# A second matrix of filter taps, with rows of 16, for the blocks that read the first one from an odd column

## The reference

```
k = jnp.transpose(kernel, (1, 2, 0))[:, :, None, :]
y = lax.conv_general_dilated(x, k, window_strides=(1, 1), padding='SAME',
                             dimension_numbers=('NHWC', 'HWIO', 'NHWC'), feature_group_count=ch)
return x + y
```

## Time and profile before

| | |
|---|---|
| median of 3 runs | 846.07 us (845.48 to 846.51) |
| the profiled execution | 845.39 us |
| its span, first to last instruction | 843.4 us |
| TensorE, matmuls | 832.9 us busy, 99% |
| VectorE | 728.6 us busy, 86% |
| ScalarE | 617.9 us busy, 73% |
| GpSimd | 248.5 us busy, 29% |
| HBM traffic over the span | 365 GB/s |

### The profile page before, as it was taken

One profiled execution on the slowest core, in us unless ns is written; L12 is line 12 of the kernel. 1 busy time (PEld: TensorE's weight loads), 2 busy tenths in 40 slices (PEclk: granted clock), 3 DMA queues, 4 the chain that ended last, 5 costly groups with the idle time before them and its releaser, 6 DMA issues.

```text
span 843.4 us, 20670 instructions
## 1 busy us (share of the span) xinstructions
PE 832.9 (99%) x7200; PEld 832.7 (99%) x7200; DVE 728.6 (86%) x2212; ACT 617.9 (73%) x1442; POOL 248.5 (29%) x460
## 2 busy tenths in 40 slices
PE   6999999999999999999999999999999999999998
PEld 6999999999999999999999999999999999999998
DVE  6888888888888888888888888888888888888886
ACT  5777677777767777777767777776777777776775
POOL 5223322323133231322323222223223231332310
PEclk9999999999999999999999999999999999999999
DMA  9999999999999999999999999999999999999965
GB/s 375 406 422 361 372 376 362 376 358 387 368 368 370 372 377 371 362 373 378 370 365 368 369 374 371 373 371 382 365 360 380 368 370 373 369 370 376 374 265 223
DMA packets 28615, 309.29 MB, mean 367 GB/s; under 512 B 3168, under 2 KB 3296, under 8 KB 4064
## 3 DMA queue, kind: packets, MB, share of 16 engines
q1 hardware_dynamic: 28512, 307.98, 97.3%
HBM read 158.55 MB, written 149.42 MB: 365 GB/s over the span
## 4 chain that ended last, share of the span: by engine, by line
PE 99%; POOL 0%; DMA 0%; issue 0%; ACT 0%; DVE 0%; DVEq 0%
PE sums L373 66%; PE sums L369 33%; DMA first<-consts 0%; POOL matrix L228 0%; POOL expanded L217 0%; POOL taps L207 0%; POOL spare L204 0%; POOL taps L201 0%; ACT y_out L259 0%; DVE y_out L313 0%; DVEq L92 0%
## 5 line engine op out<-in xcount | busy, mean ns | idle before, releaser
L373 PE MATMUL sums<-matrix,x_high 121*128 121x240 f32 (+3 forms) x4800 | 832.4, 282 | 0.0
L373 PEld LDWEIGHTS sums<-matrix,x_high 121*128 121x128 f32 x4800 | 738.1, 192 | 0.0
L369 PE MATMUL sums<-matrix,x_low 121*128 121x240 f32 (+3 forms) x2400 | 674.6, 281 | 7.0 <-POOL matrix L228 7.0
L259 ACT ACTIVATE y_out<-sums 128x99 f32<-128x99 f32 (+6 forms) x1248 | 416.6, 379 | 216.4 <-PE sums L373 196.2
L369 PEld LDWEIGHTS sums<-matrix,x_low 121*128 121x128 f32 x2400 | 461.0, 192 | 7.0 <-POOL matrix L228 7.0
L313 DVE TENSOR_TENSOR y_out<-sums,y_out 128x60 f32<-128x60 f32 (+6 forms) x1824 | 360.1, 228 | 101.5 <-ACT y_out L259 16.2
L296 DVE TENSOR_TENSOR x_low<-x_in,x_high 121x1280 fp32r<-121x1280 f32 (+1 forms) x288 | 366.3, 1272 | 5.3 <-ACT x_high L249 2.0
L228 POOL TENSOR_TENSOR matrix<-expanded,first 121x300 fp32r<-121x300 f32 x192 | 131.5, 706 | 559.9 <-PE sums L373 559.7
L249 ACT ACTIVATE x_high<-x_in 121x1280 fp32r<-121x1280 f32 x192 | 245.0, 1276 | 5.2 <-DMA x_in<-x 5.2
L217 POOL TENSOR_TENSOR expanded<-taps,first 121x100 f32<-121x100 f32 x192 | 85.3, 464 | 7.5
L287 DVE CAST x_high<-x_in 121x640 fp32r<-121x640 f32 x96 | 47.1, 490 | 4.3 <-DMA x_in<-x 3.7
(11 more groups left out here) (2 smaller groups left out, 0.2 us busy)
## 6 DMA issues: line engine op xcount, KB each, us to landing
x_in<-x SPq DMA_DIRECT2D x95, 1600.0 KB, 10.6
y<-y_out SPq DMA_DIRECT2D x95, 1520.0 KB, 12.3
x_in<-x SPq DMA_DIRECT2D x2, 640.0 KB, 5.0
rest<-later SPq DMA_DIRECT2D x1, 1150.0 KB, 11.4
y<-y_out SPq DMA_DIRECT2D x1, 852.5 KB, 3.5
y<-y_out SPq DMA_DIRECT2D x1, 365.0 KB, 2.3
x_in<-x SPq DMA_DIRECT2D x1, 320.0 KB, 3.0
y<-y_out SPq DMA_DIRECT2D x1, 302.5 KB, 2.6
```

The source lines that it names most:

```text
L259: act.activation(outputs(c, rows, cols), sums(c, t, rows, cols), ACT.Copy).then_inc(copied, 1)
L369: pe.matmul(target, x_low[c % SLOTS][0:PIXELS, at:at + IMAGES], window(c, strip, k, slice(HIGH, HIGH + 1)).squeeze(1), start=k == tile["sq ...
L373: product = pe.matmul(target, x_high[c % SLOTS][0:PIXELS, at:at + IMAGES], window(c, strip, k, slice(part, part + 1)).squeeze(1), start=Fa ...
```

## The change

GpSimd writes a second tensor, `turned`, beside `matrix`. It holds columns 1 to 16 of each of the 15 rows, so its rows are `EVEN` = 16 elements long, and what stood at column 1 of `matrix` stands at column 0. `window()` takes `matrix` where `left` is even (squares 1 and 3) and `turned`, at `left - 1`, where it is odd (squares 0, 2 and 4: from columns 2, 0 and 0). Each channel's `matrix_step` goes up by 6 in place of 4, and TensorE waits for all six before a channel.

```diff
 ROW = 4 * TAPS
+EVEN = SQUARE + 2 * HALO + 1
 MATRIX = REACH * ROW
+TURNED = REACH * EVEN
...
         matrix = [sbuf(f"matrix{i}", [P, 2, MATRIX], F32R) for i in range(SLOTS)]
+        turned = [sbuf(f"turned{i}", [P, 2, TURNED], F32R) for i in range(SLOTS)]
...
-                    pool.wait_ge(matrix_step, 4 * GROUP * group)
+                    pool.wait_ge(matrix_step, 6 * GROUP * group)
...
             def make_matrix(c):
                 if c:
-                    pool.wait_ge(matrix_step, 4 * c)
+                    pool.wait_ge(matrix_step, 6 * c)
...
-                pool.wait_ge(matrix_step, 4 * c + 2)
+                pool.wait_ge(matrix_step, 6 * c + 2)
...
+                    shape = [PIXELS, REACH // TAPS, TAPS, EVEN]
+                    pool.tensor_tensor(
+                        turned[c % SLOTS][0:PIXELS, part, :].rearrange("p (b d q) -> p b d q", d=TAPS, q=EVEN),
+                        expanded[0:PIXELS, part, :].rearrange("p (d q) -> p d q", q=ROW)[:, :, 1:1 + EVEN]
+                        .unsqueeze(1).broadcast_to(shape),
+                        down.rearrange("p (b d) -> p b d", d=TAPS).unsqueeze(3).broadcast_to(shape),
+                        ALU.mult).then_inc(matrix_step, 1)
...
-                grid = matrix[c % SLOTS][0:PIXELS, parts, :].rearrange("p a (h w) -> p a h w", w=ROW)
+                source, row = (matrix, ROW) if left % 2 == 0 else (turned, EVEN)
+                left -= left % 2
+                grid = source[c % SLOTS][0:PIXELS, parts, :].rearrange("p a (h w) -> p a h w", w=row)
...
-                pe.wait_ge(matrix_step, 4 * (c + 1))
+                pe.wait_ge(matrix_step, 6 * (c + 1))
```

## The result

The changed kernel takes 858.14 us (median, 857.13 to 858.56) against 846.09 us before. The ratio is 1.014 with an interval of 1.0128 to 1.0152. The prediction said 825.7 us, with a range from 820.5 to 833.

What follows compares the result with a forecast made beforehand. TensorE's own pace was taken as the bound: the profiled 845.39 us, less 21.1 for faster reads, plus 1.2 at the start, gave 825.5; 825.7 us was forecast, range 820.5 to 833.

Steps and rivals of the forecast that it cites:

- What bounds the kernel: Steady state: nothing feeds TensorE too late, so its own pace, 8.65 us a channel, is the time.
- TensorE's reads: Matmuls and weight loads: reading from even columns takes a channel from 8.65 to 8.43 us, a gain of 21.1 us.
- My rival that the column is not the cause: Square 2's matmuls: something else of square 2 makes it slow, so no gain, 846.6 us; chance 0.06.
- GpSimd's instructions: Two new writes a channel on GpSimd: 0.60 us each, 115 us in all, costing nothing in the steady state.
- the cover: Next channel's matrices on GpSimd: still ready 5 us early; without this slack each channel would pay 1.20 us.
- The start: Before TensorE's first load: it waits for two more writes, 1.2 us, bounds 0.8 and 2.2 us.
- DMA: Loads and stores of a channel: the rate rises from 371 to 381 GB/s, which the queue can follow.
- The rival's "3 times in all": Rival that only part is won, 836.6 us, chance 0.08; against it, only 3 DMA waits, none after the start.
- VectorE: Its work in a channel grows by 0.08 to 7.67 us against 8.43, 0.76 us free: costs nothing.
- the cover at the banks: Seam additions free banks that TensorE wants eight tiles later, more than 4 us.
- The rival "VectorE becomes the bound": GpSimd's new writes hold VectorE for their whole length, 8.79 us a channel, 860.0 us; chance 0.03.
- the point of decision: In the VectorE rival: it decides the time from 1.06 us a channel of added VectorE work on.

Runs made afterwards that it cites:

- the grouped kernel: The changed kernel with each strip's seam additions reordered, first all along the rows, then all along the columns: 822.7 us, ratio 0.9732 to the kernel before.
- the cast on ScalarE: The changed kernel with the high part of the first strip made on ScalarE in place of VectorE: 823.09 us, ratio 0.9735.
- the run without later writes: The changed kernel, but GpSimd writes `turned` in the first two channels only and later squares read old taps: 857.77 us, ratio 1.0146.
- the run with the shifted wait: The changed kernel, `turned` written in two channels only, GpSimd also waiting for VectorE's last low part of the channel ahead: 841.75 us, ratio 0.9953.

## Why the prediction was wrong, point by point

*What bounds the kernel: right.* TensorE alone set 8.65 us. Relieving VectorE changed nothing (846.48 us), and loading GpSimd changed the start alone (847.37).

*TensorE's reads: right, and slightly undervalued.* The step said 8.43 us a channel and a gain of 21.1 us. With the other engines out of the way it is 8.40, and the grouped kernel is 23.1 us under before (845.84 on its chip), where the step and the start together had promised 19.9. Of the 3.2 us more, 2.9 are the 0.03 us a channel, and the start takes 1.3 back; what is left is within the 1.7 us by which that kernel's four executions differ (822.31 to 824.02). The forecast rests on the column. My rival that the column is not the cause would have given 846.6 there.

*GpSimd's instructions: right in the bare length, wrong in the sum.* 0.61 us where nothing is beside them, 0.60 forecast. But one of each two met a low part and took up to 1.86 us, so that they are 1.15 us on the mean and GpSimd is busy for 478 us, not 365. For TensorE the cover held: the matrices are ready about 4.8 us early (7.0 before).

*The start: about right, in part by luck.* 8.48 us in place of 6.99, 1.5 us more against 1.2 forecast. In the experiments the same writes delay the first weight load by anything from 1.0 us (7.97, the cast on ScalarE) to 2.6 us (9.60, the run without later writes), past the bound of 2.2.

*DMA: right.* 382 GB/s in the grouped kernel, 381 forecast. (The rival's "3 times in all" counts ScalarE's waits for a DMA only; the trace has two more of VectorE and one of GpSimd, all at the start.)

*VectorE: this is the step that failed.* It read: "VectorE has 728.6 / 96 = 7.59 us of work in a channel, 7.67 then, against a channel of 8.43: still 0.76 us free. It costs nothing." Busy time was taken for demand. VectorE's instructions in a channel are 23, and the shortest distance of starts seen at each of the 23 places in the kernel before adds up to 8.45 us (0.52 for the high part, 0.74 for the small low part, 2.80 for the two of 1280 columns and 4.40 for the 19 additions). So 0.20 us was free before, and at TensorE's new 8.40 us nothing is. The step put the cover at the banks at "more than 4 us" besides, and it was 2.0 to 2.1. And it had the place of the collision wrong: the small low part stayed at 0.85 us on the mean (0.91 forecast), and the high part and the last low part grew. Of the 36 us between the 822 that TensorE allows and the 858 measured, the run with the shifted wait splits off the parts: 841.75 - 822.7 = 19 us are VectorE's row of instructions with light disturbances, in a run without the new writes, and 857.77 - 841.75 = 16 us come from GpSimd's writes meeting a low part. The new writes themselves added 858.1 - 857.8, next to nothing, since they replaced one collision by another: in the changed kernel the high part and the last low part are longer by 0.12 us each, in the run without the writes the last low part by 0.22 and the high part by 0.02.

*The rival "VectorE becomes the bound": the right engine for the wrong reason, at 0.03.* Its 860.0 us is near 858.1 by accident. It priced the new instructions at 1.20 us and set the point of decision 1.06 us away; the point was passed by TensorE's own gain of 0.25. The rule on mutual exclusion (the Trainium skill, "SBUF — State Buffer", section "Who interferes with whom": the later of the two waits for a whole instruction) I had read as harmless from one row. The rows above agree with it in both directions: VectorE's low part 0.22 us longer (0.35 us of GpSimd's first write were left when it began), GpSimd's write 1.25 us longer. The one that began later paid in both, so VectorE pays only once GpSimd's write begins ahead of its low part.

*Why it came late and stayed.* TensorE ran fast until its lead over VectorE was used up: the margin at the first bank of a channel was 1.67 us in the third channel and 0.15 in the eighth, and it stayed there. Meanwhile GpSimd's first write, which in the kernel before begins some 1.64 us after the start of the last low part, moved towards that start: 1.07 us after it for the fourth channel's matrix, 0.12 for the eighth's, and from the ninth's on always ahead of it, by 0.2 to 0.9 us. From then on VectorE's low part waits too, where before only GpSimd's write had. Why the phase stays there is argued, not shown by a run of its own: GpSimd is released by TensorE's channel end, TensorE by VectorE's additions, and with no margin left that release keeps a fixed distance to VectorE's row of instructions.

## What to carry to other kernels

An engine's demand is the shortest distance from its first to its last instruction of a round when it waits for no other engine; take it from starts in the timeline, since waits on its own results count and busy time leaves them out. Before making the bounding engine faster, compute that for the next one. If the two lie within a few per cent, look also at which instructions of other engines hold it up when they meet, and by how little they miss each other now, because the new pace moves them.

## What the runs showed of the hardware

- A matmul whose moving operand is read in rows of 16 floats costs about 7.5 ns a row from columns 0 and 4 of a row of 20, and about 9.0 from columns 1, 2 and 3 (134 to 137 ns for 15 rows); even and odd do not matter. Rows of 14 cost 7.2 to 7.7 ns from columns 1 to 4. The Trainium skill, "TensorE: Matmul & The Clock Gate", section "Step-by-step: what each phase is for", lets only the number of columns count; 208 elements at 97 or 118 ns and 210 elements at 110 ns contradict that. The Trainium skill, "SBUF — State Buffer", section "Specifications (TRN2)", has lines of 16 bytes and a penalty for each new line crossed; rows of 16 agree with it (four lines or five), and rows of 14 from column 3, five lines as well, do not. Why these are spared stays open.
- So the second matrix serves square 2 alone. For the 14 wide squares 0 and 4 it changes nothing that a run here could show.
- Weight loads of 128 columns go by at 111.7 ns on the mean where nothing else is seen to hold them (single distances go down to 108), 8.38 us for 75. A matmul of 15 rows from column 0 takes 110 to 115 ns where loads are halved. So in the middle strips the two are about equal, and the grouped kernel's 8.40 us a channel lies just above the pace of the loads.
